# Row statistics of four stages taken tile by tile in the stage before

## The reference, cut to what matters

```python
# x: (2, 1024, 256) f32, so 2048 rows (tokens) of 256
x = x + L0_xattn(_layernorm(x), ctx_1024, ctx_1024, mask, ...)      # 16 heads of 16, 77 keys
x = x + L0_ffn(_layernorm(x), ...)                                  # fp8-rounded 256x256 product
x = x + L1_xattn(_layernorm(x), ctx_1024, ...)                      # 16 heads of 64, q and k normalised
x = x + L1_ffn(_layernorm(x), router_w, w1, w2)                     # 8 experts, top 2 of each row
x = x + L2_xattn(_layernorm(x), ctx_1024, ...)                      # transformer block, 3 layernorms of its own
x = x + L2_ffn(_layernorm(x), wg, w1, w3, w2)                       # 8 experts, each picks 1024 rows
x = x + L3_xattn(_layernorm(x), ctx_1024, ctx_1024, mask, ...)      # as L0, with another mask
x = x + L3_ffn(_layernorm(x), ...)                                  # int8-rounded gated feed-forward
# _layernorm: (x - mean(row)) / sqrt(var(row) + 1e-5), over the 256 numbers of a row
```

## Time and profile before

| | |
|---|---|
| median of 3 runs | 1839.04 us (1839.0, 1839.04, 1842.27) |
| the profiled execution | 1837.21 us, span 1835.4 us |
| busy share of the span | PE 81%, DVE 61%, ACT 41%, POOL 35% |
| 16 `bn_stats` at a stage's head | 5.33 us, in each of the four stages |
| heads of the four stages (DVE's first instruction) | 173.73, 488.92, 1153.97 and 1720.94 us |

### The profile page before, as it was taken

How to read it: one execution, slowest core, us unless ns; L and a number is a source line. 1 busy time by engine, 2 the same in 40 slices (tenths; PEclk the granted TensorE clock), 3 DMA queues, 4 the chain that set the end, 5 groups by cost and what they waited for, 6 DMA issues and landing times. The chain is left out here.

```text
span 1835.4 us, 25274 instructions
## 1 busy us (share of the span) xinstructions
PE 1489.0 (81%) x9496; PEld 1248.7 (68%) x9506; DVE 1128.6 (61%) x2410; ACT 746.3 (41%) x1292; POOL 650.9 (35%) x406
## 2 busy tenths in 40 slices
PE   5896288999796999995798996738999996889464
PEld 3685177888565999995577775517888885578322
DVE  6386865786554776773546453576676652566567
ACT  2343364443205677672445332103333331244355
POOL 3241215556302555552113222112656564433000
PEclk8798589999967999997799998678999998789677
DMA  5000000000116777763200000312545444100101
GB/s 173 1 1 5 1 1 1 1 1 1 64 43 222 216 228 220 215 201 68 70 1 1 1 1 0 128 40 75 96 96 110 92 69 81 40 1 1 48 0 46
DMA packets 93967, 122.01 MB, mean 66 GB/s; under 512 B 12092, under 2 KB 79063, under 8 KB 93847
## 3 DMA queue, kind: packets, MB, share of 16 engines
q1 hardware_dynamic: 72727, 91.56, 15.4%
q0 software_dynamic: 21120, 28.85, 8.7%
HBM read 94.95 MB, written 25.43 MB: 66 GB/s over the span
## 5 line engine op out<-in xcount | busy, mean ns | idle before, releaser
L1169 POOL DMA_INDIRECT t_total<-t_y,t_index x46 | 99.6, 2166 | 139.3 <-DVE t_y L1290 129.2
L2452 POOL DMA_INDIRECT ch_total<-ch_y,ch_index x64 | 103.8, 1622 | 122.9 <-DVE ch_y L2631 107.9
L3337 POOL TENSOR_TENSOR L_s<-L_s,L_mx 128x1232 f32<-128x1232 f32 x32 | 77.3, 2415 | 140.9 <-DVE L_mx L3380 140.9
L732 PE MATMUL t_ps<-t_hT_hi,t_w_hi 128*128 128x256 f32 x368 | 106.8, 290 | 7.5 <-DVE t_w_lo L1278 6.0
L2571 ACT ACTIVATE ch_silu<-ch_ps 128x512 f32<-128x512 f32 x64 | 38.3, 598 | 176.8 <-PE ch_ps L734 175.1
L732 PE MATMUL ch_ps<-ch_hT_hi,ch_w_hi 128*128 128x512 f32 x256 | 104.0, 406 | 7.5 <-DVE ch_hid L2657 4.1
L733 PE MATMUL t_ps<-t_hT_lo,t_w_hi 128*128 128x256 f32 x368 | 105.9, 288 | 0.0
L734 PE MATMUL t_ps<-t_hT_hi,t_w_lo 128*128 128x256 f32 x368 | 105.8, 288 | 0.0
L732 PE MATMUL t_ps<-t_w_hi,t_act_hi 128*128 128x256 f32 x368 | 105.8, 287 | 0.0
L734 PE MATMUL t_ps<-t_w_hi,t_act_lo 128*128 128x256 f32 x368 | 104.2, 283 | 0.0
L733 PE MATMUL t_ps<-t_w_lo,t_act_hi 128*128 128x256 f32 x368 | 104.1, 283 | 0.0
(11 more groups left out here) (523 smaller groups left out, 4521.7 us busy)
## 6 DMA issues: line engine op xcount, KB each, us to landing
t_w_in<-in_L_ffn_w1T SPq DMA_DIRECT2D x23, 1024.0 KB, 4.9
t_w_in<-in_L_ffn_w2T SPq DMA_DIRECT2D x23, 1024.0 KB, 5.7
ch_w_in<-in_L_ffn_w SPq DMA_DIRECT2D x24, 512.0 KB
x<-in_x SPq DMA_DIRECT2D x1, 2048.0 KB, 8.1
t_total<-x SPq DMA_DIRECT2D x1, 2048.0 KB
t_rows<-t2d_h SPq DMA_DIRECT2D x1, 2048.0 KB
x<-t_total SPq DMA_DIRECT2D x1, 2048.0 KB, 8.3
tb_w<-in_L_xattn_w SPq DMA_DIRECT2D x2, 1024.0 KB, 11.2
```

The source lines that it names most:

```text
L732: nc.tensor.matmul(out, sh, mh, start=start, stop=False)
L1169: nc.gpsimd.indirect_dma_start(out=total, out_offset=bass.IndirectOffsetOnAxis(ap=index[:, 2 * j + u:2 * j + u + 1], axis=0), in_=y[:, j % ...
L2452: nc.gpsimd.indirect_dma_start(out=total, out_offset=at(s, u), in_=y[:, s % 2, u, :], in_offset=None, compute_op=ALU.add).then_inc(added[s ...
L3337: nc.gpsimd.tensor_tensor(s[:, n % G], s[:, n % G], spread(mx[:, n % G, :], 2, [P, H, KEYS]), ALU.subtract).then_inc(shifted, 1)
```

## The change

The 16 `bn_stats` of the four heads go away; what stays there is a new helper, `row_moments` (aggregate, eps, inverse square root). Each attention loop and the transformer block gets a `next_statistics` step that takes a finished tile's `bn_stats` into a shared tile `k.st`, and the stage ends only when all 16 are there (`next_ready`).

```diff
@@ wide_attention (narrow_attention the same, with n - 2)
+            def next_statistics(n):
+                dve.wait_ge(out_added, n + 1)
+                nc.vector.bn_stats(k.st[:, n, :], k.x[:, n, :]).then_inc(next_ready, 1)
...
                 if n + 7 < NT:
                     rows_rest(n + 7)
+                if n:
+                    next_statistics(n - 1)
             add(NT - 1)
-            dve.wait_ge(out_added, NT)
+            next_statistics(NT - 1)
+            dve.wait_ge(next_ready, NT)
@@ fp8_product, dispatch_to_tiles, choose_tokens, int8_feed_forward
-            for t in range(NT):
-                chain(nc.vector.bn_stats(st[:, t, :], k.x[:, t, :]))
-            chain.wait_apart()
...
+            row_moments(nc, chain, range(NT), k.st, mv, var, rstd, tmp)
@@ transformer_block
+            def next_statistics(g):
+                b, t0 = unit(g)
+                dve.wait_ge(x_added, g + 1)
+                for u in range(DUO):
+                    t = b * BT + t0 + u
+                    nc.vector.bn_stats(k.st[:, t, :], k.x[:, t, :]).then_inc(next_ready, 1)
...
                 if a < UNITS:
                     sum_self(a)
-            dve.wait_ge(x_added, UNITS)
+                if 1 <= g:
+                    next_statistics(g - 1)
+            next_statistics(UNITS - 1)
+            dve.wait_ge(next_ready, NT)
@@ narrow_attention, the loop
                 if n + AHEAD < NT:
                     take(n + AHEAD)
+                if n >= 2:
+                    next_statistics(n - 2)
                 if a.beside and 1 <= n <= a.beside.DVE_STEPS:
                     a.beside.centre(dve, n - 1)
...
             divide(NT - 1)
             add(NT - 2)
+            next_statistics(NT - 2)
             add(NT - 1)
-            dve.wait_ge(out_added, NT)
+            next_statistics(NT - 1)
+            dve.wait_ge(next_ready, NT)
@@ program
+        k.st = sb("st", [P, NT, 6])
```

More of the change, by code:

```diff
@@ L153, in wide_attention @@
         wide_select_ready, quarter_ready, dve_chain = sem("wide_select"), sem("quarter"), sem("dve_chain")
+        next_ready = sem("next_ready")
         block = ctx.enter_context(nc.Block())
@@ L2159, in choose_tokens @@
     mx, den = sb("mx", [P, NT]), sb("den", [P, NT])
-    st, mv = sb("st", [P, NT, 6]), sb("mv", [P, NT, 2])
+    mv = sb("mv", [P, NT, 2])
     var, rstd, tmp, pad = sb("var", [P, NT]), sb("rstd", [P, NT]), sb("tmp", [P, NT]), sb("pad", [P, 1])
@@ L2262, in _ @@
             chain = Chain(dve, chain_sem, 0, pad[:])
-            row_statistics(nc, chain, dve, k.x, range(NT), st, mv, var, rstd, tmp)
+            row_moments(nc, chain, range(NT), k.st, mv, var, rstd, tmp)
             for t in range(NT):
@@ L3034, in row_statistics, with row_moments @@
     chain.wait_apart()
+    row_moments(nc, chain, tiles, st, mv, var, rstd, tmp)
+def row_moments(nc, chain, tiles, st, mv, var, rstd, tmp):
     for t in tiles:
```

6 lines of the change are left out of this document (3 added, 3 removed).

## The result

The changed kernel takes 1845.0 us (median of 20 executions, 1835.1 to 1855.3) against 1839.5 for the kernel before on the same chip (1828.9 to 1845.2). The ratio is 1.0044, 95% interval 1.0025 to 1.0064: some 8 us slower, where I had forecast 8 us faster. The profiled execution, 1835.05 us with a span of 1833.3, is the fastest of the 20, so its length is no guide; its stages are read beside those of a second profile.

| | L0 | fp8 | wide | top-2 | transf.

The account below looks back on a forecast made before the run. It took the engine waited for at each head as the bound, DVE spending 5.33 us on sixteen `bn_stats`. Gains of 11.0 less costs of 3.2 gave 7.8 us: 1829.4 profiled, forecast 1831, range 1826 to 1836.

Parts of the forecast that it names:

- L0: First narrow attention's loop: added `bn_stats` between maximum and weight preparation is covered by DVE's 0.75 us wait; cost 0 us.
- the signs that I had named: Signs of a wrong forecast: loop `bn_stats` over 0.45 us, longer passes, or transposes that still wait for DVE.
- Rival 1: Attention loops: POOL's subtraction holds the new `bn_stats`, price 20 us, 1851 or more; chance 0.04.
- The rule against the change: Skill pages on shared POOL/DVE memory interfaces: a `bn_stats` could be held by POOL; a profile row said not.
- fp8 head: Start of the fp8 stage: 5.4 us less on DVE, less 0.9 load wait; gain 4.4 us, bounds 3.8 and 5.3.
- int8 head: Start of the int8 stage: DVE earlier, ACT's last load does not move; gain 4.3 us, bounds 2.8 and 4.5.
- Choosing head: Start of the choosing stage: PE's 32 fillers end the wait, not DVE; gain 0 us, bounds 0 and 1.1.
- Top-2 head: Start of the top-2 stage: transposes start at the fillers' end, router product sooner; gain 2.3 us, bounds -0.4 and 4.1.
- rival 3: Top-2 stage's start: fillers begin on a low clock, that term becomes -0.4, gain 5.1, 1834 us; chance 0.15.
- Wide attention: Its loop: new `bn_stats` right ahead of `take`, one of three on the path; cost 0.45 us, bounds 0 and 1.3.
- Transformer: Next to last pass: two `bn_stats` between sum and layernorm cost 0.6 us; 0.8 more at the stage's end.
- Tails: Stage ends: barrier waits for last `bn_stats`, 0.45 us in three stages, 0.8 in the transformer; cost 2.15 us.

Follow-up runs that it names:

- the run with the short delay: One `bn_stats` over 128 columns of a constant ahead of each weight-preparation step in the L0 loop, against the kernel before: 1849.8 us, ratio 1.0046.

## Why the prediction was wrong

- *What failed:* in "What is added", "L0: the added one stands between the maximum and the weight preparation ... Both leave room for 0.33 ... 0 us". I counted DVE's time and not what starts ahead of what. The cover of 0.75 us was there (a `bn_stats` in a pass with a reduction leaves 0.42 of it); the step behind it lost 1.94. Of the signs that I had named, it was the longer passes that came, with the `bn_stats` themselves at 0.42. Measured 12.7 us for a 0, which alone turns -8 into +5; the measured ratio gives +8 (4.6 to 11.8).
- *Rival 1*, POOL holds DVE, had the right mechanism and the wrong victim: it held the `bn_stats` (which POOL never held, 0.42 us everywhere), and the row that I put against it, a `bn_stats` at its usual pace and a TENSOR_SCALAR of 3.35 us behind it, was in truth the row for it. It should have made me ask, for every place where a `bn_stats` goes in, which DVE operation now starts later and what POOL does then. The trace of before had the answer in three rows: POOL's 3.16 us at 117.33 beside 2.25 at 105.72, and the second L106 of that loop, 2.32 us where its twin took 1.22. I had read a pass with a reduction, one of four; the other nine steps are of the kinds that can be held.
- *The rule against the change:* the runs have it in both directions, 1.22 to 3.16 us on DVE when POOL is first and 2.25 to 3.16 on POOL when DVE is. The Trainium skill states it in "SBUF — State Buffer", section Who interferes with whom: "Issue order, not op shape, decides who blocks", for a DVE instruction in a two-port mode, or for one with two SBUF inputs against a GpSimd instruction that reads SBUF. The trace agrees. By the same section of the Trainium skill a DVE instruction with at most one SBUF input and outside these modes does not contend. The trace agrees for TENSOR_REDUCE (1.20 and 1.21 us) and for `bn_stats` (0.42). I had cited two other pages of the Trainium skill, on whether a `bn_stats` is held, and not this one on the order.
- *fp8 head:* expected 4.4, with 0.9 of wait. Wait 0.72; L868 stands 4.40 behind the start instead of 8.96: 4.56. The stage is 4.2 shorter over all profiles. Right.
- *int8 head:* expected 4.3, from ACT's last load that "does not move". It did: 9.93 us behind the stage's start instead of 8.94, so the maximum over the rows comes 3.56 sooner (14.17 against 17.73). The 17.73 is itself long; the four other profiles with the old head have 17.36 or 17.37, which makes it 3.2. Inside the bounds of 2.8 and 4.5. The stage as a whole is 109.7 instead of 114.0 us (medians), 4.3; that this meets the forecast is luck, since what stands behind the maximum varies between 94.7 and 97.0 us, with either head.
- *Choosing head:* expected 0. The fillers bind, as expected, but took 9.00 instead of 9.58 and end 0.6 earlier; the stage median is 1.0 shorter. Right within the bound of 1.1.
- *Top-2 head:* expected 2.3, with the transposes directly behind fillers of 6.85. The transposes do follow the fillers. In the first profile the router product starts 9.60 us behind the stage's start instead of 12.08, 2.5, and the stage is 3.7 under the old median (374.1 against 377.8). But four of six profiles have the fillers of *rival 3*, given 0.15: 8.54 to 8.77 us, transposes 9.14 or 9.15 us behind the stage's start, only 0.4 earlier than the 9.54 of before, and a stage of 376.5 to 376.7, 1.2 less. In all five profiles with the old head they took 6.85. The rival had the clock down when the fillers start; it fell inside them. So the forecast's case is the rarer one of the six, and the -0.4 put down for the other was too low: 1.2 by the stage.
- *Wide attention:* 0.45 for one of three places, measured 0.8 with the tail taken off (medians of the stage 262.6 and 261.4), as if two of them were on the path. That is not shown pass by pass, and the profiles of one kernel differ by 1.2 and more. Inside the bound of 1.3.
- *Transformer:* 0.6 + 0.8. From the next to last sum to the next stage 11.87 instead of 10.62: 1.25. Right.
- *Tails:* 0.45 each; the L0 tail is 2.05 us from the last addition to the next stage instead of 1.56: 0.49. Right.

Without the L0 loop the forecast of -7.8 stands against -5.1 (-8.6 to -1.5) for the run with the `bn_stats` behind the step, and about -7 by the medians of the stages, tails included. The heads and the tails were sized about right, the top-2 head with luck in part.

## What to carry to other kernels

Where POOL and DVE both worked from SBUF here, it was the order in which their operations started that decided which of the two was held (1.22 us or 3.16 for one DVE step), and 0.2 us of new DVE work turned it. So before an instruction goes in, list the next DVE operation, ask whether it is a copy, a tensor-scalar or one of two SBUF tiles, and look at what starts on POOL within a few tenths of a microsecond. Put new work behind the operation that has to start first, or let the engine with slack wait. The hint in a trace is one operation with two durations.

## What was not expected of the hardware

- A held L100, 1.22 us by itself, ends 1.08 us behind POOL's operation (121.07 against 119.99; in the run with the short delay 123.81 against 122.73). The 0.18 us step L97 ends 0.05 behind it (113.83 against 113.78): held steps lose POOL's remaining time, less some 0.14 us.
- A lead of 0.12 us was enough for DVE to be first, and one of 0.04 us for POOL.
- Four memsets of one column in a row delayed the DVE step behind them by about 0.03 us together.
- The same 31 fillers took 6.85 or 8.5 to 8.8 us in profiles of one kernel, with the granted clock full when they started and, in the second case, at half in their second and third microsecond.
- Kernels with the same timing in their traces came out at 0.9973 and 0.9985 of the kernel before.
